# Cross attention with RMS-normed keys: keys made with the head dimension on partitions, and their roots put onto the scores

## The reference

```python
q = (hidden_states @ Wq).reshape(B, Sq, H, D)          # hidden_states: layernorm(x), 16 x 100 x 512
k = (encoder_hidden_states @ Wk).reshape(B, Skv, H, D)  # 16 x 361 x 256, H = 16 heads of D = 128
v = (encoder_hidden_states @ Wv).reshape(B, Skv, H, D)
q = rmsnorm(q, gq)          # x * rsqrt(mean(x^2) + 1e-5) * g, over D
k = rmsnorm(k, gk)
scores = jnp.einsum('bqhd,bkhd->bhqk', q, k) * scale
attn = jax.nn.softmax(scores, axis=-1)
out = jnp.einsum('bhqk,bkhd->bqhd', attn, v).reshape(B, Sq, H * D)
x = x + out @ Wo            # then x = x + ffn(layernorm(x)), weights from 4-bit codes
```

## Time and profile before

| | |
|---|---|
| median of 3 runs | 1964.02 us (1962.7 to 1964.23) |
| the profiled execution | 1964.5 us, of which the span of the trace is 1962.7 us |
| PE busy | 1941.3 us, 99% |
| DVE, ACT, POOL busy | 81%, 50%, 55% |
| mean granted TensorE clock | 0.999 |
| last scores of the attention | start at 1154.2 us |

### The profile page before, as it was taken

The page is one execution under the profiler, slowest core; times in us unless marked ns, Lnnn a source line. Parts: engine busy times, 40 slices in busy tenths (PEclk is TensorE's granted clock), DMA queues, the critical chain, the costliest instruction groups (busy, mean ns, idle before and its releaser), DMA issues.

```text
span 1962.7 us, 33387 instructions
## 1 busy us (share of the span) xinstructions
PE 1941.3 (99%) x11276; PEld 1850.4 (94%) x11276; DVE 1586.2 (81%) x2990; ACT 983.1 (50%) x2275; POOL 1074.4 (55%) x1211
## 2 busy tenths in 40 slices
PE   8999999999999999999999999999999999999999
PEld 7899899999999999999999999988999999999999
DVE  6888877787877787887878887888888888888875
ACT  4655555555555455555545543444444444444442
POOL 5755555412423322334222335888888888878871
PEclk9999999999999999999999999999999999999999
DMA  6434443433433333333223333211111111111101
GB/s 212 135 120 156 161 139 116 134 100 91 132 113 96 124 101 114 102 120 118 94 95 116 114 101 109 66 33 44 33 33 33 33 33 33 33 33 33 33 1 68
DMA packets 93512, 174.53 MB, mean 89 GB/s; under 512 B 13264, under 2 KB 49760, under 8 KB 91296
## 3 DMA queue, kind: packets, MB, share of 16 engines
q1 hardware_dynamic: 93344, 172.39, 27.2%
HBM read 139.00 MB, written 33.36 MB: 88 GB/s over the span
## 4 chain that ended last, share of the span: by engine, by line
PE 88%; DVE 5%; POOL 3%; issue 2%; ACT 1%; DMA 1%; SPq 0%; DVEq 0%; ACTq 0%; POOLq 0%
PE psum L420 43%; PE psum L794 19%; PE psum L451 6%; PE psum L484 4%; PE psum L508 4%; PE psum L514 3%; PE psum L509 3%; PE psum L493 3%; PE psum L524 1%; PE psum L569 1%; POOL inter_lo L1981 1%; PE psum L575 0%; DVE ysum L1497 0%; DVE g L1464 0%; DVE work L1347 0%
## 5 line engine op out<-in xcount | busy, mean ns | idle before, releaser
L1838 POOL TENSOR_SCALAR k_ss<-k_ss 122x4 f32<-122x4 f32 x192 | 37.2, 194 | 423.3 <-DVE k_ss L1300 423.2
L899 ACT ACTIVATE work<-psum,stats,q_rstd 100x361 f32<-100x361 f32 x256 | 163.8, 651 | 177.6 <-DVE stats L1338 177.6
L1244 DVE TENSOR_TENSOR kaT_lo<-psum,kaT_hi 128x488 fp32r<-128x488 f32 (+2 forms) x384 | 214.1, 613 | 45.2 <-ACT kaT_hi L842 45.1
L420 PE MATMUL psum<-wk,ctxT_hi 128*122 128x512 f32 x768 | 242.0, 396 | 0.0
L1981 POOL TENSOR_TENSOR inter_lo<-g,inter_hi 128x400 fp32r<-128x400 f32 x127 | 143.1, 1132 | 126.1 <-ACT inter_hi L842 125.3
L842 ACT CAST kaT_hi<-psum 128x488 fp32r<-128x488 f32 (+2 forms) x384 | 178.7, 540 | 57.9 <-PE psum L493 57.8
L1840 POOL TENSOR_TENSOR k_ss<-k_ss,power 122x4 f32<-122x4 f32 x192 | 193.9, 1010 | 16.0
L420 PE MATMUL psum<-inter_hi,down_hi 128*128 128x400 f32 x512 | 176.1, 344 | 3.2 <-POOL inter_lo L1981 1.6
L1330 DVE TENSOR_REDUCE stats<-psum 100x2 f32<-100x722 f32 x128 | 115.9, 905 | 75.0 <-PE psum L451 75.0
L420 PE MATMUL psum<-inter_lo,down_hi 128*128 128x400 f32 x512 | 175.5, 343 | 0.0
L420 PE MATMUL psum<-inter_hi,down_lo 128*128 128x400 f32 x512 | 175.3, 342 | 0.0
(11 more groups left out here) (260 smaller groups left out, 5939.5 us busy)
## 6 DMA issues: line engine op xcount, KB each, us to landing
head_w<-spill_sq SPq DMA_DIRECT2D x48, 512.0 KB, 3.5
head_w<-spill_so SPq DMA_DIRECT2D x46, 512.0 KB, 3.8
wk<-spill_sk SPq DMA_DIRECT2D x12, 1024.0 KB, 4.9
wv<-spill_sv SPq DMA_DIRECT2D x48, 256.0 KB, 2.8
spill_so<-head_w SPq DMA_DIRECT2D x16, 512.0 KB, 3.0
spill_sq<-head_w SPq DMA_DIRECT2D x14, 512.0 KB, 3.0
wk_raw<-in_ctxT SPq DMA_DIRECT2D x12, 361.0 KB, 4.2
spill_sk<-wk SPq DMA_DIRECT2D x4, 1024.0 KB, 6.0
```

Of the source, the lines that this page charges most:

```text
L420: last = e.matmul(out, a_, b_, start=begins and i == 0, stop=ends and i == len(passes) - 1)
L899: e.activation(attn[h][:, 0:SKV], bank[3 + h][0:SQ, 0:SKV], ACT.Exp, bias=st[:, h:h + 1], scale=rq[:, i * QH + h:i * QH + h + 1], accum_ou ...
L1244: e.tensor_tensor(dst, src, high.bitcast(F32), ALU.subtract).then_inc(S[sem], 1)
```

## The change

Keys are now made one head at a time with the head dimension on partitions: `keys(u, h)` is 6 matmuls with wk as the stationary operand and 362 columns of ctxT, 24 matmuls for a unit, into banks 0, 1, 2 and 7. They need no transposes and are split at once into hi and lo (`key_hi`, `key_lo`), unnormalised; head 3 has buffers of its own (`k3T`). The root of each key goes another way. ScalarE squares the four heads into `k_sq`; TensorE sums over partitions with the strip of ones (`keys_summed`, 4 fp32 matmuls into bank 7); ScalarE copies the sums out (`key_sums_evicted`); a DMA spreads 4 rows of 372 over 124 partitions of 12 (`gather_sums`); GpSimd takes the power on 124 x 12; a second DMA stores it to DRAM (`store_roots`), and a third reads it back to all of 100 partitions (`spread_roots`, 100 x 1488). In the next unit VectorE multiplies the scores by it and takes the maximum in the same instruction (`scaled`, one head at a time), after which one more instruction changes the sign; ScalarE's exponentials now read and write SBUF.

Scores are made in the order of heads 3, 0, 1, 2, with `keys_summed` ahead of head 2. The keys of the next unit now stand ahead of the scores, and the fillers are dealt out anew. `key_order` puts head 3's key product last where bank 7 comes free late: in units with i = 1 and i = 3 from unit 5 on, in unit 0, and in units 4, 12, 24, 28, 40, 44 and 56.

```diff
-                scores(u)
-                if u == 0:
-                    squares_summed(0, 7)
-                for t in range(KT):
-                    keys(u + 1, t)
...
+                for n, h in enumerate(key_order(u + 1)):
+                    keys(u + 1, h)
...
+                scores(u, 3)
+                scores(u, 0)
+                scores(u, 1)
+                keys_summed(u + 1, 7)
+                if i == 3 and more and quad > 0:
+                    e.wait_ge(S["mx"], 4 * u + 1)
+                    squares_summed(quad + 1, 6)
+                scores(u, 2)
+
+                if i == 3 and quad > 0 and more:
+                    e.wait_ge(S["ksv"], u + 2)
+                    output(quad - 1, 2, 7)
+                else:
+                    e.wait_ge(S["mx"], 4 * u + 1)
+                    if quad == 0:
+                        query(1, i, 6, (0, 1))
+                    elif i == 0:
+                        value_of(quad - 1, 0, 6)
+                        e.wait_ge(S["ksv"], u + 2)
+                        value_of(quad - 1, 1, 7)
+                    elif more:
+                        query(quad + 1, i, 6)
+                    else:
+                        output(quad - 1, 2 * i - 2, 6)
 
                 transpose_attn(u)
...
-            def transpose_keys(u, t):
-                e.wait_ge(S["khat"], 3 * u + t + 1)
+            def keys_summed(u, into):
...
+                e.wait_ge(S["ksq"], 4 * u + QH)
+                e.wait_ge(S["kTl"], 4 * u + 1)
                 for h in range(QH):
...
+                    last = e.matmul(bank[into][cols(h, STRIP), 0:SCOLS], strip[:, :], k_sq[:, h, :], start=True, stop=True)
+                last.then_inc(S["kss"], 1)
...
+                for h in key_order(u + 1):
+                    square_key(u + 1, h)
+                    if h == 3:
+                        key_hi(u + 1, h)
+                exponential(u, 3)
+                exponential(u, 0)
+                key_sums_evicted(u + 1, 7)
+                exponential(u, 1)
+                if i == 3 and more and quad > 0:
+                    squares_evicted(quad + 1, 6)
+                exponential(u, 2)
...
+            def key_hi(u, h):
+                if h < QH - 1 and u > 0:
+                    e.wait_ge(S["y"], 2 * u)
...
+            def scaled(u, h):
+                st, rq = stats[u % 2], q_rstd[u // GB % 2]
+                at = u % GB * QH + h
+                if h == ORDER[0]:
+                    e.wait_ge(S["d_kb"], 16 * (u + 1))
...
+                e.wait_ge(S["sc"], 4 * u + RANK[h] + 1)
+                e.tensor_tensor_reduce(out=attn[h][:, 0:SKV], in0=bank[3 + h][0:SQ, 0:SKV], in1=key_root[:, h * SPAN:h * SPAN + SKV],
+                                       scale=rq[:, at:at + 1], scalar=LOWEST, op0=ALU.mult, op1=ALU.max,
+                                       accum_out=st[:, h:h + 1]).then_inc(S["mx"], 1)
+                e.wait_ge(S["mx"], 4 * u + RANK[h] + 1)
+                e.tensor_scalar(st[:, h:h + 1], st[:, h:h + 1], -1.0, None, ALU.mult).then_inc(S["neg"], 1)
...
+                key_lo(u + 1, 3)
+                scaled(u, 3)
+                scaled(u, 0)
+                scaled(u, 1)
+                normalise_attn(u, 3)
+                scaled(u, 2)
+                normalise_attn(u, 0)
+                normalise_attn(u, 1)
+                normalise_attn(u, 2)
...
+            def gather_sums(u):
+                e.wait_ge(S["ksv"], u + 1)
+                load(k_root[:, :], k_sums[0:(QH - 1) * STRIP + 1:STRIP, :], "d_kr")
+
+            def store_roots(u):
+                e.wait_ge(S["krs"], u + 1)
+                load(d["kr"], k_root[:, :], "d_kd")
+
+            def spread_roots(u):
+                e.wait_ge(S["d_kd"], 16 * (u + 1))
+                if u > 0:
+                    e.wait_ge(S["mx"], 4 * u)
+                load(key_root[:, :], d["kr"].rearrange("p n -> (p n)").unsqueeze(0).broadcast_to([SQ, QH * SPAN]), "d_kb")
```

618 lines of the change are left out of this document (304 added, 314 removed).

## The result

The changed kernel takes 2023.24 us (median of 4 runs, 2015.47 to 2024.0) against 1963.74 (1962.7 to 1964.23) for the kernel before on the same chip: ratio 1.0295, 95% interval 1.0269 to 1.032. It is **slower by 59.5 us, 3%**. The forecast was 1978 with a range up to 2015: the sign is right, but the forecast slowdown of 14 us is a quarter of the measured one.

What follows compares the result with a forecast made beforehand. The prediction took TensorE to bound the kernel. From 1964.5 us: -36 saved work, +39 waits in 14 quads, +4 later units, +4 quad 0, +1 quad 15, +5.5 unit 0, -3.7 absorbed idle, giving 1978 us; range 1948 to 2015.

Steps and rivals of the forecast that it cites:

- What bounds the kernel: TensorE, busy 1941.3 of 1962.7 us: a matmul removed saves its full time, a new wait costs its full time.
- 50 to 55 forecast: Expected idle time of TensorE in the attention, in us, most of it before transposes of the softmax.
- TensorE's own work, -0.56 a unit: Key matmuls and transposes removed, less new key matmuls and strip sums: -0.56 us a unit, -36 us over 64.
- the second wait there: At i = 2, head 0's key split takes 1.27 us after `attend` against 0.99 of key product: 0.25 us.
- The links: VectorE's four `scaled` of 0.80 and `normalise_attn` of 0.52 take 5.36 us; TensorE waits 2.81 us a quad, +39.
- rival A: VectorE's links are shorter and the saving shows: 1930 to 1961 us, 27%.
- 0.74 for the point where waits and saving cancel: Length of one `scaled`, about 0.74 us, that decides between the forecast and rival A.
- Hidden, by 1.7 us: At i = 1 the roots arrive at 15.6 us, ahead of the next `scaled` at 17.3, so transfers cost nothing.
- rival B: The roots come late and hold VectorE's queue at the first `scaled`: 2008, up to 2040 us, 17%.
- +4 for quad 0 and +5.5 for unit 0, 3.3 of it for the first roots: Opening: half a filler in three units, +4 us; unit 0's late order 2.2 and first roots some 3.3, +5.5.
- the forecast's 6: Forecast loss in us for units 4 to 62: 39 + 4 + 1 less 34, less 4 that move to the start.
- What would show it: Signs expected in the trace after, among them no VectorE wait on the DMA of `key_root` behind unit 0.

Runs made afterwards that it cites:

- x12: x10 with VectorE's product over only the first 180 of 361 columns of each head: 1970.45 us.
- x10: Changed kernel without the spread of the roots and VectorE's wait for it, scores multiplied by a constant; gather, root and store kept: 1990.54 us.
- x14: Changed kernel whose spread carries only head 3's roots, 145 of 581 KB, with every wait kept: 1993.92 us.
- x1: Changed kernel without the three root transfers and GpSimd's root; scores multiplied by a constant written once: 1994.24 us.
- x7: x1 with the new group's first query product put behind two key products in units 12, 28 and 44: 1993.83 us.
- x13: x1 with the splits of the normalised tokens ahead of those of the next unit's keys in units 12, 28 and 44: 1993.99 us.
- x9: x6 with the spread of the roots cut into two transfers, head 3's piece first: 2033.69 us.
- x2: Changed kernel with the 122x2x256 load of raw context rows written as two loads of 122x256: 2012.79 us.
- x6: Changed kernel with the raw context rows of batches 2 and 3 loaded behind unit 1's spread: 2013.07 us.
- x16: Changed kernel with two GpSimd split steps in the first four units moved ahead of the root of the next unit's keys: 2010.61 us.
- x5: x2 with GpSimd's own queue issuing gather, store and spread instead of SyncE's: 2063.74 us.

## Why the prediction was wrong

- **What bounds the kernel: right.** A wait that TensorE hadn't had costs its time; idle time grew by 35 us in the steady part. Its 59 us in the attention are near the 50 to 55 forecast by chance: 23 of them stand in the first four units.
- **TensorE's own work, -0.56 a unit: right.** -0.54 at i = 2, where nothing waits. (The forecast's own terms give 1.27 - 0.99 = 0.28 for the second wait there, not 0.25; neither came.)
- **The links: right mechanism, too long.** `scaled` is 0.70, not 0.80; the read of the accumulator (0.083) and the sign overlap. Waits in a quad are 1.6 us (2.24 of saving less 0.61), not 2.81; at i = 1 they are near the forecast's where nothing covers them (unit 17). x12 shows the mechanism at work. With 0.70 an undisturbed unit is rival A, and that a clean quad gains 0.61 fits its 0.74 for the point where waits and saving cancel. The overlap of 0.08 us, which the prediction set against the Trainium skill's rule on the drain, shows in unit 37 too: the next `scaled` starts at 737.91, the sign ahead of it ends at 737.99. That doesn't refute the skill: the same section ("The DRAIN you can't avoid" of "VectorE: DVE Perf Modes") adds that a next instruction that is not held starts earlier, which the prediction left out.
- **"Hidden, by 1.7 us": this step failed, and with it the forecast.** In a clean unit it holds. But 2.3 for a gather and 3.9 for the spread were taken from medians of a kernel whose transfers had room; where VectorE waited, the spread took 5.3 to 8.7, and gathers took up to 9.0. The slack should have been held against the worst unit. That is rival B: 23.0 us in the steady part (30.2 less x10's 7.2), 32.7 in all, with x14 showing that the bytes do it. That B's "2008, up to 2040" holds the 2023 is in part luck, since 11 us of unit 1 are GpSimd's wait and what stands behind it, which B didn't count.
- **"+4 for quad 0 and +5.5 for unit 0, 3.3 of it for the first roots": failed, by 19 us.** Units 0 to 3 took 21.4 more: 5.7 are there without any roots (x1), where TensorE stands 6.0 us in units 0 and 1 ahead of transposes of the softmax, for VectorE's products and scalings; 13.8 with gather, root and store (x10), where GpSimd stands at the gather with TensorE's splits behind it; 21.4 with the spread. In unit 1 alone it is 3.6, 14.4 and 22.1. Nothing in the text named what is queued behind GpSimd's wait, nor looked at how long SyncE's queue was held (12.99 us, in the trace of before).
- **Normalising units: missed.** About 3 us each in three units, 8.8 in all in x10; x7 and x13 only moved it. That the cover of the key transposes is gone there is argued, no run shows it. So x10's 7.2 in the steady part lies near the forecast's 6 by luck: clean quads came out about 1 us shorter each than forecast, the units around a normalisation longer.
- **What would show it.** "No wait of VectorE on the DMA of `key_root` behind unit 0; if there is one, it is B": there were 13, so this sign was a good one.

Still open: why one transfer in two pieces costs 20 us (x9), and why the steady part is 4 to 10 us shorter in x2, x6 and x16, whose edits have no reason to act there.

No version tried beats the kernel before. The best that computes the same is x16, 2010.6; even with free roots (x10) it is 1990.5. A clean quad gains 0.61 us. Sixteen of them would be 10 us, an estimate that no run bears out: x10's steady part is 7.2 us longer than before.

## What to carry to other kernels

A transfer that replaces work is only hidden if its slowest instance fits, beside the largest reload and in the opening, not its median in a kernel that had less to move; so count the bytes that the new path adds (211 MB on the queue against 172 before) and hold them against the fullest unit. Ask of every wait that a change adds what is queued behind it on its engine; here GpSimd's mattered as much in the opening as VectorE's. And an ablation that frees an engine also moves its work: x1 and x10 differ by 4 us in all, but by 8 us one way in the first four units and by 11 the other way behind them.

## What the runs showed of the hardware

- VectorE's in-place scaling of 100x361 in SBUF takes 0.41 us, and 1.25 beside a GpSimd subtraction of 128x512 (x1, rows above), up to 1.98 elsewhere in x1; the product from PSUM keeps its 0.575 to 0.595. The Trainium skill ("SBUF — State Buffer", section "🔬 SBUF: two separate sides") has a pair of ports shared by the two engines; whichever of a GpSimd instruction and a VectorE instruction in a mode of two ports starts first holds it for the whole instruction. The trace fits this, though no row tells the scaling's mode: it ends at 131.91, 0.21 us after the subtraction.
- In the changed kernel four issues of context rows held SyncE's queue for 13.6 us in issuing, six smaller ones of the same bytes 13.5 (x2), while 1 MB of key weights is issued in 0.3 (`752.66 0.33` in unit 38).
- Behind 18.2 us of idle time TensorE's granted clock was 0.50 (1.2 GHz), and its first 8.5 us of work ran at that: some 4 us on top of the wait itself.
- The same spread of 581 KB lands after 4.1 us in the median of x5 and released VectorE after 5.3 to 8.7 where that waited in the changed kernel; a gather of 6 KB released GpSimd after 1.9 to 9.0.
